# First cross attention of a Perceiver block: the product of the query and key weights, made on the chip, in place of two products of the tokens

## The reference, cut to what matters

```
q = xn @ Wq.T + bq            # 1024 x 512
k = ctx @ Wk.T + bk           # 257 x 512 per batch
s = q @ k.T / sqrt(512)       # then a mask-free softmax over the 257 keys
x = x + softmax(s) @ (ctx @ Wv.T + bv)
```

## Time and profile before

| | us |
|---|---|
| median of three runs | 1789.21 |
| lowest and highest of them | 1784.83, 1790.46 |
| profiled execution | 1792.57 |
| its span, first to last instruction | 1789.6 |
| PE busy in it | 1646.7 (92%) |
| DVE, ACT busy | 944.2 (53%), 646.1 (36%) |

### The profile page before, as it was taken

One profiled execution on the slowest core, in us unless ns is written; L12 is line 12 of the kernel. 1 busy time (PEld: TensorE's weight loads), 2 busy tenths in 40 slices (PEclk: granted clock), 3 DMA queues, 4 the chain that ended last, 5 costly groups with the idle time before them and its releaser, 6 DMA issues.

```text
span 1789.6 us, 37879 instructions
## 1 busy us (share of the span) xinstructions
PE 1646.7 (92%) x16852; PEld 1329.1 (74%) x16852; DVE 944.2 (53%) x1376; ACT 646.1 (36%) x1139; POOL 190.8 (11%) x168
## 2 busy tenths in 40 slices
PE   4988888999899899998999999999989998899996
PEld 3733776888677688876888888888867777677885
DVE  4331764433526665472555555555555156558886
ACT  2211145222433411113333333333342511338882
POOL 1200330000100000012000000000003000064331
PEclk9989878999899999999999999999989979999998
DMA  5198100111010011102111111111120200069995
GB/s 210 60 348 324 43 24 24 60 58 58 19 56 3 26 48 56 59 27 76 39 55 55 55 53 48 51 49 37 37 70 9 75 4 4 25 223 377 410 405 195
DMA packets 60673, 172.57 MB, mean 96 GB/s; under 512 B 7280, under 2 KB 24192, under 8 KB 50016
## 3 DMA queue, kind: packets, MB, share of 16 engines
q1 hardware_dynamic: 53536, 153.86, 23.9%
q0 software_dynamic: 3664, 10.27, 1.5%
q10 hardware_dynamic: 3312, 6.03, 0.9%
HBM read 151.68 MB, written 18.39 MB: 95 GB/s over the span
## 4 chain that ended last, share of the span: by engine, by line
PE 80%; DVE 10%; issue 5%; ACT 3%; POOL 1%; DMA 1%; SPq 0%; ACTq 0%; DVEq 0%; POOLq 0%
PE PS L790 22%; PE PS L791 21%; PE PS L792 21%; PE PS L1166 2%; PE PS L897 2%; PE PS L1135 2%; PE PS L1021 2%; PE PS L918 1%; PE PS L1168 1%; DVE bns L1706 1%; PE PS L1150 1%; PE PS L1263 1%; DVE Wl L1771 1%; PE PS L1035 1%; PE PS L805 1%
## 5 line engine op out<-in xcount | busy, mean ns | idle before, releaser
L790 PE MATMUL PS<-T1h,Wh 128*128 128x512 f32 x512 | 209.2, 409 | 23.6 <-DVE T1l L1784 11.7
L791 PE MATMUL PS<-T1l,Wh 128*128 128x512 f32 x512 | 206.6, 404 | 0.0
L792 PE MATMUL PS<-T1h,Wl 128*128 128x512 f32 x512 | 206.3, 403 | 0.0
L1637 POOL TENSOR_TENSOR rs<-ve,half 128x1 f32<-128x1 f32 (+1 forms) x64 | 46.8, 731 | 1389.8 <-DVE ve L1721 1058.6
L1771 DVE TENSOR_TENSOR Wl<-W,Wh 128x2048 fp32r<-128x2048 f32 x45 | 103.1, 2291 | 96.1 <-ACT Wh L1312 96.1
L790 PE MATMUL PS<-CTh,Wh 128*128 128x256 f32 x512 | 148.3, 290 | 0.6 <-ACT SCP L1510 0.6
L791 PE MATMUL PS<-CTl,Wh 128*128 128x256 f32 x512 | 144.8, 283 | 0.0
L792 PE MATMUL PS<-CTh,Wl 128*128 128x256 f32 x512 | 144.8, 283 | 0.0
L790 PEld LDWEIGHTS PS<-T1h,Wh 128*128 128x128 f32 x512 | 100.8, 197 | 46.8 <-DVE T1l L1784 12.8
L790 PE MATMUL PS<-Wh,B1h 128*128 128x512 f32 x336 | 132.9, 396 | 0.0
L2127 DVE COPY pool_area<-PS 128x512 f32<-128x512 f32 x64 | 44.3, 692 | 165.6 <-PE PS L792 165.6
(11 more groups left out here) (334 smaller groups left out, 3462.4 us busy)
## 6 DMA issues: line engine op xcount, KB each, us to landing
W<-units_dram SPq DMA_DIRECT2D x54, 1024.0 KB, 5.9
pool_area<-units_dram SPq DMA_DIRECT2D x19, 1024.0 KB, 8.2
pool_area<-ctx_t_dram SPq DMA_DIRECT2D x32, 512.0 KB, 4.0
T1f<-ctx_dram SPq DMA_DIRECT2D x25, 512.0 KB, 6.8
SCP<-units_dram SPq DMA_DIRECT2D x9, 1024.0 KB, 8.5
H<-ctx_t_dram SPq DMA_DIRECT2D x15, 516.0 KB, 8.0
T1f<-ctx_t_dram SPq DMA_DIRECT2D x12, 516.0 KB, 7.5
xs_dram<-pool_area SPq DMA_DIRECT2D x23, 256.0 KB, 2.4
```

Of the source, the lines that this page charges most:

```text
L790: nc.tensor.matmul(out_, a[0], b[0], start=first, stop=False)
L791: nc.tensor.matmul(out_, a[0], b[1], start=False, stop=False)
L792: return nc.tensor.matmul(out_, a[1], b[0], start=False, stop=last)
L1637: nc.gpsimd.tensor_tensor(rs[:, t, 0:n], ve[:, t, 0:n], half[:, 0:n], ALU.pow).then_inc(power_ready, 1)
```

## The change

Group 0 is normalized and transposed as before. Then PE makes `wr`, the rows Wq.T @ bk and bq @ Wk: eight float32 matmuls whose stationary operand is one column of bias and whose moving operand is a raw (unsplit) chunk of a weight, 128 x 512. It makes `M` from the pairs of Wq and Wk (48 matmuls), turns the rows into columns (`wc`, eight small transposes and one matmul for bq . bk), transposes group 1, and makes `qk` directly from `T1` and the pair `Mh`, `Ml`. Both products `q` are gone, with their drains. Wk is now split at the start. SP loads tiles 4 to 7 of x behind the weights and constants, and the buffers that share memory with `T1` (contexts 4 to 6) and, behind two of them in the queue, unit 3, after the last `qk`. The transposes for `c` now stand in the middle of `qk` of group 1.

```diff
@@ plan()
-        for m in range(C):
-            J.add(("q", g, m), "dve", unit="0.wq", split=True)
+        if g == 0:
+            J.add(("wr",), "act", banks=2)
+            for m in range(C):
+                J.add(("M", m), "dve", unit="0.wq", split=True)
+            J.add(("wc",), "dve")
...
@@ SP
             def load_ct(i):
                 if i == CT_EARLY:
-                    sp.wait_ge(ready, J.ready["q", G - 1, C - 1])
+                    sp.wait_ge(ready, J.ready["qk", G - 1, C - 1])
...
             for i in range(CT_EARLY):
                 load_ct(i)
+            sp.wait_ge(ready, J.ready["wr",])
             load_unit(2)
...
@@ PE
-            for g in range(G):
-                for t in range(g * TG, g * TG + TG):
-                    transpose_tile("t1", t, xn, XNB["t1"])
-                w = wait_unit("0.wq")
-                wait(("t1", g * TG + TG - 1))
-                feature_major(("q",), w, T1, g)
-            wait(("q", G - 1, C - 1))
+            for t in range(TG):
+                transpose_tile("t1", t, xn, XNB["t1"])
+
+            pe.wait_ge(w_full[0], 16)
+            pe.wait_ge(w_full[1], 16)
+            pe.wait_ge(biases_ready, 1)
+            wait_banks(("wr",))
+            bk = banks(("wr",), 2)
+            for i, b in enumerate((key_bias, v_("bq0"))):
+                for c in range(C):
+                    mm = nc.tensor.matmul(bk[0:1, i, :], b[:, c:c + 1], W[:, i, c, :], start=(c == 0), stop=(c == C - 1))
+            mm.then_inc(ready, 1)
+
+            wq, wk = wait_unit("0.wq"), wait_unit("0.wk")
+            for m in range(C):
+                wait_banks(("M", m))
+                for c in range(C):
+                    mm = split_product(banks(("M", m)), cut(wq, slice(None), c, slice(m * P, (m + 1) * P)),
+                                       cut(wk, slice(None), c, slice(None)), c == 0, c == C - 1)
+                mm.then_inc(ready, 1)
...
+            for t in range(TG, T):
+                transpose_tile("t1", t, xn, XNB["t1"])
+            wait(("M", C - 1))
+            w = Mh, Ml
+            feature_major(("qk",), w, T1, 0)
+            wait(("t1", T - 1))
             pe.wait_ge(small_split, 1)
-            per_token_rows("crow", B1, "bk0")
-            w = wait_unit("0.wk")
-            feature_major(("qk",), w, B1, 0)
+            per_token_rows("crow", T1, "bk0")
+            feature_major(("qk",), w, T1, 1, [0, 1])
             per_token("c", "crow", 1)
-            feature_major(("qk",), w, B1, 1)
+            feature_major(("qk",), w, T1, 1, [2, 3])
...
@@ DVE
+            dve.wait_ge(const_in, 16 * 9)
+            link(nc.vector.memset(ones, 1.0))
+            nc.vector.tensor_tensor(both_biases, key_bias, v_("bq0"), ALU.mult).then_inc(biases_ready, 1)
             split_low(0)
+            split_low(1)
...
             for m in range(C):
-                low(("q", 0, m), B1, (A_, m, grp(0)), bias=v_("bq0")[:, m:m + 1])
+                low(("M", m), (Mh, Ml), (A_, m, A_))
+            dve.wait_ge(ready, J.ready["wc",])
+            step(nc.vector.tensor_copy(key_bias, banks(("wc",))[:, 0:C]))
+            step(nc.vector.tensor_copy(qk_bias, banks(("wc",))[:, C:2 * C]))
+            fence()
+            nc.vector.reduce_sum(c_bias, banks(("wc",))[:, 2 * C:3 * C], AX_X).then_inc(dve_drained, 1)
```

More of the change, by code:

```diff
@@ L665, in _ @@
             sp.dma_start(cst[:, :], con).then_inc(cst_in, 16)
-            for t in range(T):
+            for t in range(TG):
                 sp.dma_start(X[:, t, :], x[t]).then_inc(x_in[t], 16)
-            sp.dma_start(vec[:, :, :], vecs).then_inc(const_in, 16)
             load_unit(0)
             load_unit(1)
+            sp.dma_start(vec[:, :, :], vecs).then_inc(const_in, 16)
             sp.dma_start(scl[:, :], scalars.rearrange("(o r) -> o r", o=1).to_broadcast([P, NSCL])).then_inc(const_in, 16)
@@ L866, in _ @@
             pe.wait_ge(cst_in, 16)
-            for g in range(G):
-                for t in range(g * TG, g * TG + TG):
-                    transpose_tile("t1", t, xn, XNB["t1"])
-                w = wait_unit("0.wq")
-                wait(("t1", g * TG + TG - 1))
-                feature_major(("q",), w, T1, g)
-            wait(("q", G - 1, C - 1))
+            for t in range(TG):
+                transpose_tile("t1", t, xn, XNB["t1"])
[9 more added lines that the diff above has]
+            wq, wk = wait_unit("0.wq"), wait_unit("0.wk")
+            for m in range(C):
+                wait_banks(("M", m))
[3 more added lines that the diff above has]
+                mm.then_inc(ready, 1)
+            wait(("wr",))
+            wait_banks(("wc",))
+            bk = banks(("wc",))
+            for n in range(2 * C):
+                nc.tensor.transpose(bk[:, n:n + 1], bias_rows[:, n * P:(n + 1) * P], ident[0:1, 0:1])
+            nc.tensor.matmul(bk[:, 2 * C:3 * C], ones, both_biases, start=True, stop=True).then_inc(ready, 1)
+            for t in range(TG, T):
+                transpose_tile("t1", t, xn, XNB["t1"])
[3 more added lines that the diff above has]
+            wait(("t1", T - 1))
             pe.wait_ge(small_split, 1)
-            per_token_rows("crow", B1, "bk0")
-            w = wait_unit("0.wk")
-            feature_major(("qk",), w, B1, 0)
+            per_token_rows("crow", T1, "bk0")
+            feature_major(("qk",), w, T1, 1, [0, 1])
             per_token("c", "crow", 1)
-            feature_major(("qk",), w, B1, 1)
+            feature_major(("qk",), w, T1, 1, [2, 3])
             def values_up(v):
@@ L1315, in next_after, with drain_features @@
                 split_high(UNIT[name] + NW)
-            def drain_features(name, dst, scale=1.0, groups=range(G)):
+            def drain_features(name, dst, scale=1.0, groups=range(G), bias=None):
                 for g in groups:
@@ L1321, in drain_features @@
                         act.wait_ge(ready, J.ready[name + (g, m)])
+                        if bias is not None:
+                            nc.scalar.activation(dst[:, m, grp(g)], banks(name + (g, m)), ACT.Identity,
+                                                 bias=bias[:, m:m + 1]).then_inc(act_drained, 1)
+                            continue
                         nc.scalar.activation(dst[:, m, grp(g)], banks(name + (g, m)), ACT.Copy, scale=scale).then_inc(act_drained, 1)
@@ L1380, in high_values @@
                 nc.scalar.copy(T1h[:, :, tok(v)].rearrange("p h (j q) -> p j h q", j=PB), src).then_inc(high, 1)
+            high_transposes("t1", 0)
+            high_transposes("t1", 1)
             split_high(0)
[L1383 to L1394, removed]
+            high_transposes("t1", 2)
+            high_transposes("t1", 3)
+            split_high(1)
+            act.wait_ge(ready, J.ready["wr",])
+            nc.scalar.copy(bias_rows, banks(("wr",), 2)[0:1].rearrange("p n d -> p (n d)")).then_inc(act_drained, 1)
+            for m in range(C):
+                act.wait_ge(ready, J.ready["M", m])
+                nc.scalar.copy(Mh[:, m, :], banks(("M", m))).then_inc(high, 1)
+            for t in range(TG, T):
+                high_transposes("t1", t)
+            act.wait_ge(dve_drained, J.drain["wc",][1])
+            nc.scalar.copy(smh[:, :], sc[:, 0:NSPLW]).then_inc(small_high, 1)
+            drain_features(("qk",), QK, groups=[0], bias=qk_bias)
             next_after("0.wq")
@@ L1398, in _ @@
             nc.scalar.activation(scl[:, 0:2 * R + 1], scl[:, 0:2 * R + 1], ACT.Exp, scale=-1.0).then_inc(exp_ready, 1)
-            drain_features(("qk",), QK)
+            drain_features(("qk",), QK, groups=[1], bias=qk_bias)
             next_after("0.wk")
```

25 lines of the change are left out of this document (16 added, 9 removed).

## The result

The changed kernel took 1774.36 us (median of 5 runs, 1772.88 to 1778.58) against 1789.21 us of the kernel before in the same comparison: a ratio of 0.9922, 95% interval 0.9905 to 0.9940. The forecast was 1785.7, in a range of 1776.5 to 1791.5, so the time lies under the range. Over the runs of the study, single ones left out, the medians are 1775.1 (11 runs of the changed kernel) and 1789.1 (56 runs of the one before, 1778.2 to 1794.2).

The account below looks back on a forecast made before the run. It took the wait chain through `c` and DVE's 19.8 us to the softmax, then DMA, as the bound; terms put `c` at 72.9, 3.5 us earlier, so 1789.21 became 1785.7, range 1776.5 to 1791.5.

Parts of the forecast that it names:

- The start: Loads and casts before `wr`: constants at 15.7 us, bias product from 16.0, both weights' low parts beside it until 20.5.
- The bias rows: `wr` on PE: sixteen records 0.85 us apart at the lower clock, 13.6 us in all, ending at 29.7.
- the upper one: For `wr`, the bound of 13.6 us at 1.2 GHz, taken instead of the lower bound of 6.9.
- the first rival: Clock rises about 4 us into `wr`: `wr` 8.9 us, `M` 10.97, all 10.5 us earlier, 1778.7; chance 0.33.
- `M`: 48 matmuls behind `wr`: 13.2 us, the first 4.0 at the lower pace, ending at 42.9.
- if the clock is up already: For `M`, the lower bound of 11.0 us, with PE at 2.4 GHz from its start.
- From `M` to `c`: A wait of 5.3 us after `M`, `qk` starting at 48.2, and `c` at 72.9.
- the last term: From the start of `qk` to `c`: group 0 begins at the lower pace and takes 12.7 us; `c` at 72.9.
- Behind `c`: Set-up chain to the first softmax stays 19.8 us; unit 3 hidden by 3.0 us; attention starts 3.5 us earlier.
- the late unit: Rival: unit 3 shares the DMA engines with eight contexts, lands at 95.7, softmax 3.6 us later, 1792.8; chance 0.10.
- the loads that eat the gain: Rival: attention bound by bytes after `qk`, 2.6 MB more cost 6.7 us, net -2; shares the forecast's chance 0.57.
- my sum: Terms up to `c` put it at 72.9, 3.5 us earlier; the end follows one to one, giving 1785.7.

Follow-up runs that it names:

- the two executions of the first `u` above: Profiled executions of the changed kernel, 1774.36 us, and of it with 6 more dense matmuls ahead of `c`, 1777.59 us; the latter's clock stayed at 0.50 to beyond 100.
- the two repeats of the changed kernel: The changed kernel run again without alteration for a second and third profile: 1775.78 us (6 runs) and 1775.73 us (single run).
- the delays of 1.4 and 2.7 us: The changed kernel with 6 and with 12 more dense, overwritten matmuls ahead of the transposes of `c`: 1777.59 us and 1779.11 us.
- the largest: The changed kernel with 48 more dense, overwritten matmuls ahead of the transposes of `c`: 1783.80 us (8 runs), ratio 0.9958.
- the old start: The changed kernel with the order of loads and casts of the kernel before: 1778.22 us (6 runs), ratio 0.9941.
- the start alone: The kernel before with only tiles 4 to 7 of x loaded behind weights and constants, and ACT casting two tiles before Wq: 1784.70 us, ratio 0.9967.

## Why the prediction was wrong

**The start: held.** Constants at 15.7 predicted, the step behind them at 16.49; `wr` at 17.00 instead of 16.0; the low parts of both weights lay beside it.

**The bias rows: the failed step.** I had bounds of 6.9 and 13.6 and took "the upper one", because "the nearest row of thin work is L923", which had run "without the clock rising". Measured 26.50 - 17.00 = 9.5 us, the 8.9 of the first rival and a little more: the clock rose inside the line. It wasn't the chance of one execution: in the eight profiles that have these sixteen records, changed start or old, the first eight took 5.05 to 6.30 us, the second eight 3.60 in each. The row that I generalized from was one execution of a stretch that comes out either way, as the two executions of the first `u` above show; and it was thin in another sense than `wr`: both move 512 columns, but L923 fills 4 of the 128 rows and `wr` all rows with one column. The Trainium skill, TensorE: Matmul & The Clock Gate, Part 1: The HAM clock gate (the "warmup" mystery), has the gate follow how busy the engine has been and count no instructions. In `wr` the trace agrees (1057 ns falling to 592 inside one line); the first `u` and the scores behind it, busy at 0.50 to beyond 100 in the execution above, do not fit it, and I had set one such row against it.

**`M`: the same error once more.** 13.2 us predicted, the first 4.0 at the lower pace; measured 37.6 - 26.50 = 11.1, near the bound of 11.0 "if the clock is up already", and it was up.

**From `M` to `c`: held.** The gap to `qk` was 42.41 - 37.6 = 4.8 (5.3 predicted), from there to the transposes of `c` 66.11 - 42.41 = 23.7 (24.0). With the terms in a row: 1.0 later at `wr`, 4.1, 2.1, 0.5 and 0.3 less, 6.0 in all: 72.9 - 6.0 = 66.9, measured 66.81. That the last term held was chance: I let `qk` begin at the lower pace, as the second `q` had; in the two repeats of the changed kernel it began at full pace and took 22.1 us to the transposes of `c`, and `c` stood at 65.2 and 64.1.

**Behind `c`: held.** 19.8 us to the softmax in each profile; the rivals of the late unit and of the loads that eat the gain did not come about (unit 3 landed 7.3 us after its issue and was hidden by 1.9, not 3.0; the loop ran at 393 GB/s). That the end follows `c` held for the delays of 1.4 and 2.7 us within 1.4 us; of the 10.9 us of the largest, 6 to 9 came through.

**The rest: open.** With `c` 9.6 earlier my sum would have given 1779.6, with the 11.1 of the mean profiles 1778.1, and the first rival stood at 1778.7; measured were 1774.4. So of the 11.3 us by which the forecast was too high, 6 to 8 are the bias rows and the products behind them, and the other 4 to 5 belong to no term of the sum that I can name. I had reckoned each kernel from one execution, in which `c` scatters by 1 to 3 us and the stages behind the attention by 4 to 5. In the profiles 11.1 of the 13.8 us between the mean spans are `c`. In the medians, kernels with the new algebra lie some 5 us under those with the old at the same `c` (1783.8 at 76.9 against 1789.1 at 76.4; with the old start 1778.2 at 71.5, against 1784.7 at 70.3 for the start alone). A part may be the clock: the mean granted clock of the eight runs with 48 matmuls is 0.9576, of the kernel before beside them 0.9557, and by the slope over the runs of the kernel before (0.9 us per 0.001) that is an estimated 1.7 us. What holds the remainder, and in which stage, no run tells.

## What to carry to other kernels

An operation on a path that begins on an idle PE has two prices, and which applies is not read from one stretch of one execution: look for the same stretch in several profiles, or measure the operation twice over, before taking the slow price. A thin operation on the way may pay part of its cost back: behind the bias rows the first product took 11.1 us, where it took 13.2 when it was the first dense work itself. And when a gain is larger than the moved wait explains, take the distances between the same points in several profiles of both kernels before looking for a cause in the change.

## What the runs showed of the hardware

Float32 matmuls of 512 columns with a stationary operand of one column cost what those with 128 columns cost: 592 ns a record at 2.4 GHz, 0.43 to 0.44 us apart. At 1.2 GHz they took 1057 ns and stood 0.85 apart, as the records of `u` with 32 columns did.

The spread of the timed runs goes with the mean granted clock of the run: over the 51 runs of the kernel before for which it is on record in the experiments the correlation of time and clock is -0.81; runs at 0.951 to 0.953 took 1791 to 1792 us on average, those at 0.959 to 0.960 1786. In profiles with the clock lost in other places the untouched stages behind the attention took 1542.9 to 1550.5 us.
